# First bias of a top-2 mixture added on VectorE, and split expert weights kept in DRAM for the second mixture

## The reference, cut to what matters

```
logits = x @ gate_w.T + gate_b
top_vals, top_idx = top_k(logits, 2); routing = softmax(top_vals)
for e in range(8):
    h = x @ w1[e].T + b1[e]                       # 256 -> 512
    y = h[:, 0::2] * sigmoid(1.702 * h[:, 0::2]) * (h[:, 1::2] + 1.0)
    ye = y @ w2[e].T + b2[e]                      # 256 -> 256
    out = out + ye * sum(routing * (top_idx == e))
```

## Time and profile before

| | us |
|---|---|
| median of 3 runs | 2635.42 |
| lowest, highest | 2635.4, 2640.15 |
| the profiled execution, its own time | 2634.61 |
| its span, first to last instruction | 2632.8 |
| moe0: its start to the first tile | 0 to 62.02 |
| moe0: tile loop | 62.02 to 187.2 |
| moe1: its start to the first tile | 1001 to 1044.55 |
| moe1: tile loop | 1044.55 to 1173.0 |

### The profile page before, as it was taken

One profiled execution on the slowest core, in us unless ns is written; L12 is line 12 of the kernel. 1 busy time (PEld: TensorE's weight loads), 2 busy tenths in 40 slices (PEclk: granted clock), 3 DMA queues, 4 the chain that ended last, 5 costly groups with the idle time before them and its releaser, 6 DMA issues. The chain is left out here.

```text
span 2632.8 us, 44981 instructions
## 1 busy us (share of the span) xinstructions
PE 2357.4 (90%) x15959; PEld 1837.2 (70%) x15959; DVE 1699.6 (65%) x3422; ACT 1351.9 (51%) x2729; POOL 1133.2 (43%) x1015
## 2 busy tenths in 40 slices
PE   4985899999999994978989999889979999998799
PEld 3874555665666553866877777677778887886688
DVE  7548786776777716547555997879855545555443
ACT  4433345555555563433238886868655544444322
POOL 2553111211112111555316773746466677777232
PEclk9997899999999995998999999999999999999999
DMA  5224001000000003233000000000023333333200
GB/s 171 77 90 123 20 11 36 16 20 20 16 25 9 16 20 121 78 106 140 1 15 1 1 5 5 1 9 1 25 101 101 90 98 106 104 104 105 86 9 25
DMA packets 79941, 138.65 MB, mean 53 GB/s; under 512 B 27360, under 2 KB 48568, under 8 KB 78832
## 3 DMA queue, kind: packets, MB, share of 16 engines
q0 software_dynamic: 26512, 74.12, 9.4%
q1 hardware_dynamic: 53216, 61.65, 7.4%
HBM read 114.53 MB, written 20.94 MB: 51 GB/s over the span
## 5 line engine op out<-in xcount | busy, mean ns | idle before, releaser
L1634 ACT ACTIVATE PT<-ps 128x512 f32<-128x512 f32 (+3 forms) x640 | 300.5, 535 | 269.3 <-PE ps L1354 268.6
L2618 POOL DMA_INDIRECT KV<-kv_scratch,sidx x288 | 275.2, 956 | 113.4 <-issue 90.2
L35 PE MATMUL ps<-KIh,qih 128*128 128x512 f32 (+2 forms) x640 | 246.5, 385 | 45.9 <-DVE Isc L2118 35.3
L1496 DVE TENSOR_REDUCE xn<-ps 128x1 f32<-128x512 f32 x384 | 243.1, 684 | 67.8 <-PE ps L1339 65.6
L2181 POOL TENSOR_TENSOR part_sum<-part_sum,rlp 128x1024 f32<-128x1024 f32 (+7 forms) x138 | 241.0, 1746 | 95.8 <-ACT rlp L2011 94.7
L36 PE MATMUL ps<-KIl,qih 128*128 128x512 f32 (+2 forms) x640 | 239.3, 374 | 0.0
L37 PE MATMUL ps<-KIh,qil 128*128 128x512 f32 (+2 forms) x640 | 238.9, 373 | 0.0
L2118 DVE SCALAR_TENSOR_TENSOR Isc<-ps,iw,Isc 128x1024 f32<-128x1024 f32 (+7 forms) x198 | 191.9, 969 | 56.4 <-ACT ps L2035 52.8
L2035 ACT ACTIVATE ps<-ps,iwa 128x1024 f32<-128x1024 f32 (+7 forms) x222 | 188.0, 864 | 33.8 <-PE ps L37 33.4
L35 PEld LDWEIGHTS ps<-KIh,qih 128*128 128x128 f32 x640 | 124.3, 194 | 87.2 <-issue 65.8
L931 POOL TENSOR_TENSOR fyl<-fy,fyh 128x512 fp32r<-128x512 f32 x64 | 84.9, 1327 | 183.8 <-ACT fyh L811 183.8
(11 more groups left out here) (397 smaller groups left out, 6802.9 us busy)
## 6 DMA issues: line engine op xcount, KB each, us to landing
cs<-in_rope SPq DMA_DIRECT2D x20, 512.0 KB, 4.2
ycomb<-y_rows SPq DMA_DIRECT2D x16, 512.0 KB, 5.5
w1raw<-in_w SPq DMA_DIRECT2D x14, 512.0 KB, 5.5
KV<-kv_scratch,sidx POOLq DMA_INDIRECT x288
w2raw<-in_w SPq DMA_DIRECT2D x14, 256.0 KB, 6.4
xn_rows<-xnr SPq DMA_DIRECT2D x5, 512.0 KB, 4.9
wir<-in_wi SPq DMA_DIRECT2D x1, 2176.0 KB, 10.3
X<-in_x SPq DMA_DIRECT2D x1, 2048.0 KB
```

The costliest lines, as they stand in the source:

```text
L35: pe.matmul(out, lhs[0], rhs[0], start=start, stop=False)
L1496: v.tensor_reduce(part, o, AX_X, ALU.max).then_inc(a_free, 1)
L1634: s.activation(PT[:, rnd % 2, hh, lo:CH], ps[:, BANK[kind, u, j, r, hh % 2], lo:CH], ACT.Exp, scale=SCALE).then_inc(a_exp, 1)
L2618: g.indirect_dma_start(ring(k, m), None, a["kv_scratch"], bass.IndirectOffsetOnAxis(sidx[:, t % 2, at:at + 1], 0)).then_inc(rows_in[k % RB ...
```

## The change

It has two parts. **The first bias on DVE.** The matmul L703 goes. The bias b1 is transposed once (n == 0), stored as eight rows of 512 (`bias_up`), and in each mixture a DMA on SP spreads all eight rows to every partition (`bb1`, 16 KB a partition, 2 MB). In the loop DVE adds `bb1` of the tile's expert to the 512 columns in PSUM and writes `ub` in SBUF; DVE reads the expert's number with a register load of its own. The sigmoid, gt and y then read `ub` instead of PSUM. PE's U waits for `ub` of two tiles earlier instead of y. In the loop ACT does yh ahead of sig, and DVE does xgl, ub, yl, gt, y. `bb` holds only b2, so ACT clears 2048 elements instead of 6144, and the split and the bias rows have 256 elements instead of 768.

**The last four experts kept.** In moe0's loop SP stores the high and low parts of w1 and w2 of experts 4 to 7 to DRAM: four DMAs of 2, 2, 1 and 1 MB in rows of 16, 16, 8 and 8 KB a partition, the first behind result 4, the others 7 results apart. In moe1 experts 4 to 7 are not loaded raw, cast or subtracted; POOL issues four DMAs that read the kept parts back, right behind `ln_root` and ahead of its wait for the bias rows. PE's wait for low parts covers four experts (`whole_low`), and its wait `m_bg` also covers the kept parts (`pool_in`).

```diff
+        ub = sb("ub", [P, 2, F1], F32, moe_ctx)
-        gt = sb("gt", [P, 2, I], F32, moe_ctx)
-        y = sb("y", [P, 2, I], F32, moe_ctx)
+        gt, y = ub[:, :, 0:I], ub[:, :, I:F1]
...
+        def keeps(n):
+            return n == 0 and begun(1) > 0
+        def whole_low(n):
+            return E * (n + 1) if not begun(n) else E * n + WR + 1
+        def pool_in(n):
+            return 32 * (n + 1) + 64 * sum(begun(m) > 0 for m in range(n + 1))
+        def small_in(n):
+            return 64 * (n + 1) + 64 * sum(keeps(m) for m in range(n))
...
# SP, behind the stores of the rows and of bhi and blo
+            if n == 0:
+                sp.wait_ge(m_b1, 18)
+                sp.dma_start(b1_d, b1row[:]).then_inc(m_b1, 16)
+                sp.wait_ge(m_b1, 34)
+            sp.dma_start(bb1[:].rearrange("p e f -> p (e f)"), b1_d.rearrange("e f -> (e f)").partition_broadcast(P)).then_inc(m_b1, 16)
             for e in range(WR + 1, E):
-                weights(e)
+                if not begun(n):
+                    weights(e)
+            if keeps(n):
+                sp.wait_ge(m_wl, E * (n + 1))
+                for m, (kept, w) in enumerate(((kept1_d, w1h), (kept1_d, w1l), (kept2_d, w2h), (kept2_d, w2l))):
+                    sp.wait_ge(m_os, NT * n + 4 + 7 * m)
+                    sp.dma_start(kept[m % 2].bitcast(F32), w[:, WR + 1:].bitcast(F32)).then_inc(m_b, 16)
+                sp.wait_ge(m_b, small_in(n) + 64)
...
# ACT's loop: yh is put ahead of sig
+                    s.wait_ge(m_ub, 2 * A - 1)
+                    s.activation(sig[:, k % 2, :], ub[:, k % 2, 0:I], ACT.Sigmoid, scale=1.702).then_inc(m_sig, 1)
...
# DVE's loop
+                    if k == 0:
+                        v.wait_ge(m_b1, 34 + 16 * (n + 1))
+                        v.wait_ge(m_rt, routed("expert", n))
+                    e = v.value_load(te_u[0:1, k:k + 1], min_val=0, max_val=E - 1)
+                    v.wait_ge(m_up, A)
+                    if k >= 2:
+                        v.wait_ge(m_yt, A - 2)
+                    v.tensor_tensor(ub[:, k % 2, :], ps[:, U_BANK + k % 2, :], bb1[:, bass.ds(e, 1), :].rearrange("p a f -> p (a f)"),
+                                    ALU.add).then_inc(m_ub, 1)
# (yl)
+                    v.wait_ge(m_sig, A)
+                    v.tensor_tensor(gt[:, k % 2, :], ub[:, k % 2, 0:I], sig[:, k % 2, :], ALU.mult).then_inc(m_ub, 1)
+                    v.wait_ge(m_ub, 2 * A)
+                    v.scalar_tensor_tensor(out=y[:, k % 2, :], in0=ub[:, k % 2, I:F1], scalar=1.0, in1=gt[:, k % 2, :],
+                                           op0=ALU.add, op1=ALU.mult).then_inc(m_y, 1)
...
# POOL, behind ln_root
+            if begun(n):
+                for m, (kept, w) in enumerate(((kept1_d, w1h), (kept1_d, w1l), (kept2_d, w2h), (kept2_d, w2l))):
+                    g.dma_start(w[:, WR + 1:], kept[m % 2]).then_inc(m_bg, 16)
...
# PE
-            pe.wait_ge(m_wl, E * (n + 1))
-            pe.wait_ge(m_bg, 32 * (n + 1))
+            pe.wait_ge(m_wl, whole_low(n))
+            pe.wait_ge(m_bg, pool_in(n))
...
-                    pe.wait_ge(m_y, max(A - 2, 0) if r >= 2 else NT * n)
+                    pe.wait_ge(m_ub, 2 * (A - 2) - 1 if r >= 2 else 2 * NT * n)
...
-                    pe.matmul(o, selr[:], bb[:, bass.ds(e, 1), 0:F1].rearrange("p a f -> p (a f)"), start=False, stop=True).then_inc(m_up, 1)
+                    j.then_inc(m_up, 1)
```

More of the change, by code:

```diff
@@ L244, in build @@
         b1raw = sb("b1raw", [P, E, F1 // P], F32, share)
+        b1row = sb("b1row", [E, F1], F32, share)
         b2raw = sb("b2raw", [E, D], F32, share)
-        bhi = sb("bhi", [E, F1 + D], F32R, share)
-        blo = sb("blo", [E, F1 + D], F32R, share)
+        bhi = sb("bhi", [E, D], F32R, share)
+        blo = sb("blo", [E, D], F32R, share)
         share.close()
@@ L268, in build @@
         w1_dram, w2_dram = a["w1"], a["w2"]
+        kept1_d = nc.dram_tensor("kept_w1", (2, P, E - WR - 1, KD, F1), F32R, kind="Internal").ap()
+        kept2_d = nc.dram_tensor("kept_w2", (2, P, E - WR - 1, JI, D), F32R, kind="Internal").ap()
         m_w, m_wh, m_wl = [sem(f"m_w{k}") for k in range(WR + 1)], sem("m_wh"), sem("m_wl")
-        (m_b, m_bb, m_bg, m_io, m_rp, m_ra, m_rt, m_row, m_tr, m_xh, m_xl, m_up, m_sig, m_gt, m_y, m_yt, m_yh, m_yl, m_dn, m_os, m_x) = (
-            sem(x) for x in ("m_b m_bb m_bg m_io m_rp m_ra m_rt m_row m_tr m_xh m_xl m_up m_sig m_gt m_y m_yt m_yh m_yl m_dn m_os m_x").split())
+        (m_b, m_b1, m_bb, m_bg, m_io, m_rp, m_ra, m_rt, m_row, m_tr, m_xh, m_xl, m_up, m_sig, m_ub, m_y, m_yt, m_yh, m_yl, m_dn, m_os, m_x) = (
+            sem(x) for x in ("m_b m_b1 m_bb m_bg m_io m_rp m_ra m_rt m_row m_tr m_xh m_xl m_up m_sig m_ub m_y m_yt m_yh m_yl m_dn m_os m_x").split())
         m_rows = [sem("m_rows0"), sem("m_rows1")]
@@ L352, in moe_scalar @@
             s.wait_ge(consts, FIRST_IN)
[L353 to L357, removed]
+            s.activation(bb[:].rearrange("p e f -> p (e f)"), ident[:, 0:1].to_broadcast([P, E * D]), ACT.Copy, scale=0.0).then_inc(m_bb, 1)
+            s.wait_ge(m_b, small_in(n))
+            s.copy(bhi[:], b2raw[:]).then_inc(m_bb, 1)
+            if n == 0:
+                s.wait_ge(m_b1, 17)
+                s.copy(b1row[:], ps[0:E, CNT_BANK, :]).then_inc(m_b1, 1)
             for c in range(begun(n), NCH):
                 q = NCH * LNC[n] + c
-                if c >= 2:
-                    s.wait_ge(m_rp, PRODUCTS * n + c)
+                if c >= begun(n) + 2:
+                    s.wait_ge(m_rp, PRODUCTS * n + c - 1)
                 for k in range(KD):
@@ L370, in moe_scalar @@
             s.activation(gate[:], gap[:], ACT.Sigmoid).then_inc(m_ra, 1)
-            s.wait_ge(m_rp, PRODUCTS * n + NCH + 2)
+            s.wait_ge(m_rp, PRODUCTS * n + NCH + 1)
             s.copy(totb[:], ps[:, CNT_BANK, 0:1].to_broadcast([P, P])).then_inc(m_ra, 1)
-            for e in range(WR + 2 - (begun(n) > 0), E):
-                weights(e)
+            for e in range(WR + 2, E):
+                if not begun(n):
+                    weights(e)
             for i in range(NT + 3):
@@ L381, in moe_scalar @@
                     s.copy(xgh[:, i % 2].rearrange("p k t -> p (k t)"), ps[:, T_BANK + i % 2, 0:D]).then_inc(m_xh, 1)
[L382 to L386, removed]
                 if 2 <= i < NT + 2:
@@ L640, in logits @@
                                       start=t == CT * begun(n) and k == 0, stop=t == TILES - 1 and k == KD - 1)
[L641 to L646, removed]
+                i.then_inc(m_rp, 1 + (begun(n) if c == NCH - 1 else 0))
+            pe.wait_ge(m_b, small_in(n))
+            if n == 0:
+                pe.wait_ge(m_b1, 16)
+                for j in range(F1 // P):
+                    i = pe.transpose(ps[0:E, CNT_BANK, j * P:(j + 1) * P], b1raw[:, :, j], ident[:])
+                i.then_inc(m_b1, 1)
             for c in range(begun(n), NCH):
@@ L722, in moe_tensor @@
                                  w2l[:, bass.ds(e, 1), h, :].rearrange("p a f -> p (a f)")), h == 0, False)
-                    pe.matmul(o, selr[:], bb[:, bass.ds(e, 1), F1:F1 + D].rearrange("p a f -> p (a f)"), start=False, stop=True).then_inc(m_dn, 1)
+                    pe.matmul(o, selr[:], bb[:, bass.ds(e, 1), :].rearrange("p a f -> p (a f)"), start=False, stop=True).then_inc(m_dn, 1)
         ahead_ctx = ExitStack()
```

45 lines of the change are left out of this document (21 added, 24 removed).

## The result

The changed kernel takes **2660.19 us** (median of 4 runs, 2656.98 to 2663.47), the kernel before 2635.84 on the same chip (4 runs). The ratio is 1.0087, with a 95% interval of 1.0071 to 1.0102. I had forecast 2638.4 and a range of 2621 to 2653, so the result is outside the range on the slow side.

A forecast was written before the change was run, and what follows sets the result against it. The prediction took PE to bound both tile loops. From the profiled 2634.6 us, plus 0.8 to the median, it added -11 + 5.3 + 1.2 + 7.5 = +3.0, giving 2638.4 us, range 2621 to 2653.

The forecast's parts named there:

- What bounds the loop: Both tile loops: PE busy 120.6 of 125.2 and 121.6 of 128.5 us, so PE bounds; 2.88 us a tile.
- Part 1, -11: Both loops without the bias matmul: tile from 2.88 to near 2.74 us (estimates 2.65, 2.79, 2.72); -11 us.
- POOL: Loops: DMAs starting at random moments wait for DVE operations with two SBUF operands, 0.14 us a tile, giving 2.72.
- rival D: Loops: POOL's scatter meets gt or y in every tile, 3.0 us a tile, no gain; 2649.4 us, chance 0.17.
- Part 2, +5.3: moe0's loop: stores delay gathers, packets alternating one for one; 2.4 us per 2 MB store, 0.25 per 1 MB; +5.3.
- Part 3, +1.2: moe0's start: storing and spreading b1 moves expert 4's landing from 33.9 to 39.4; +1.2 us (0 to +6.4).
- E: moe0's start: the spread of b1 runs at half rate, +5.2 us; total 2643.6 us, chance 0.13.
- Part 4, +7.5: moe1's start: kept loads pass before expert 3, which comes 15.0 us later; first tile +7.1, second gather +0.4; +7.5 us.
- The variant with turns of 4 KB: moe1's start: kept parts get 4 KB a turn, expert 3 only 6.5 us later; 2629.9 us, chance within B's 0.24.
- B: moe1's start: rings favour SP's queue or share by bytes, -6.6 for +7.5; 2624.3 us, chance 0.24 with the 4 KB variant.
- C: Loops: PE stays the bound at 2.65 us a tile, gathers' slack takes the stores; 2626.1 us, chance 0.10.
- The rest, 0: The span outside moe0 and moe1: carried over unchanged, 0 us.

The follow-up runs named there:

- run 6: Kernel before, with TensorE's register load of a tile's expert number moved from behind T to behind the previous tile's U; 2628.34 us, ratio 0.9962.
- run 1: Changed kernel without the kept experts, so the bias part alone; 2641.11 us, ratio 1.002 to the kernel before.
- run 5: run 1 with TensorE's register load of the expert number moved behind the previous tile's U; 2626.29 us, ratio 0.9953 to the kernel before.
- run 10: Changed kernel with the edits of run 3, run 5 and run 7, and POOL issuing gathers ahead of the result wait and scatter; 2607.16 us, ratio 0.988.
- run 12: run 10 without the kept part; 2615.46 us, ratio 0.9892 to the kernel before.
- run 11: run 10 without the bias part, the first bias again by TensorE's product; 2618.1 us, ratio 0.9909 to the kernel before.
- run 2: Kernel before with only the kept part added, bias still a matmul; 2658.58 us, ratio 1.0099.
- run 4: Changed kernel with each store cut by expert into rows of 4 and 2 KB, pieces still issued together; 2660.13 us, ratio 1.0099 to the kernel before.
- run 3: Changed kernel with POOL issuing the kept loads only once expert 3's raw weights have landed; 2642.82 us, ratio 1.0024 to the kernel before.
- run 8: run 2 with the edits of run 3 and run 7, bias still a matmul; 2635.09 us, ratio 0.9982 to the kernel before.
- run 7: Changed kernel with the stores cut by expert into sixteen, one at every second result; 2651.48 us, ratio 1.0052 to the kernel before.

## Why the prediction was wrong

**What bounds the loop: wrong, and the first cause.** I read "PE is busy 120.6 of 125.2 us" as the bound and took the pace for PE's. Run 6 took 7.5 and 7.3 us out of the two loops without touching PE's work. Gaps of 0.3 to 0.7 us in some tiles are lost in a 96% share. My 2.88 us was the pace of tiles whose register load is hidden; the mean over before's loop is 120.2 / 38 = 3.16. The row that told it was in my hands, and I named the register load, but priced it as something the new chain would bring, not as what the loop already paid.

**Part 1, -11: wrong.** The step that failed is "2.65, 2.79 and 2.72 meet near 2.74". Measured in run 1: -0.6 and +0.3. I let an exposed register load cost 2.79 a tile at the worst, by a chain through Y. In run 1 tiles take 2.65 to 3.7 us, because the load starts only shortly before T, and a load that lasts 523 instead of 300 ns puts U off by that much more. PE's sequencer had lost part of its lead, as I had written, but the price was too low: the steps from T to U grew by 6.7 us in the first loop, most of the 9 us that 39 bias matmuls of 0.23 us take. That this is the cause is shown by run 5 (-6.4 and -8.8 us for the one move). The rest of the gain hung on POOL's order (runs 10 and 12). With both out of the way the part gives 6.7 and 6.6 us a loop (run 11 against 10), 13.3 in all, 0.17 a tile; so -11 was about the price of the part, but not in this kernel. The bound of 2.65 us a tile that I had given PE alone is what runs 10 and 12 reach. DVE's register load, which I counted as nothing, takes 0.30 us and 0.19 for the arithmetic in run 10, and the tiles of 2.65 us run all the same.

**POOL: the wait right, its timing and size wrong.** I had a scatter or gather meet DVE's operations with two SBUF operands at random. The runs show it otherwise:

```profile
89.80 0.96 POOL L661 DMA_INDIRECT xg<-xn_rows,id_in  x1 [0.30 <-issue]
...
90.82 0.42 DVE L619 SCALAR_TENSOR_TENSOR ub<-ub 128x256 f32<-128x256 f32 x1
91.07 1.04 POOL L673 DMA_INDIRECT y_rows<-osb,id_out  x1 [0.30 <-issue]
```

This is run 10. In its first loop all 34 scatters that the timeline shows between 70 and 168 us start inside y (L619), as rival D had it, with 0.04 to 0.28 us of y left, and they are longer by about what is left: 1.04 us with 0.17 left, 1.15 with 0.28, 0.99 with 0.04. (The gather of 1.54 in the earlier trace rows started with 0.58 us of L406 left.) So a scatter does wait for y's end, but it comes late in y and pays 0.17 us at most, not 0.42. The gathers start outside gt and y and stay at 0.96. The means are 1.07 and 0.96, with two gaps of 0.30 that makes 2.63 a tile, just under PE's 2.65, where I had 2.72. Rival D's price (3.0 a tile, each scatter held for a whole DVE operation) is refuted: tiles of 2.65 us run through both loops of runs 10 and 12. The Trainium skill (SBUF — State Buffer, SBUF: two separate sides) has the loser of the shared port pair blocked until the other's instruction is over. The scatters' lengths agree with that; the gathers, beside which gt runs at its usual 0.42 us, show no wait on either side.

**Part 2, +5.3: mechanism half right, size too small.** The loop lost 9.4 us (9.7 in run 2). The failed step is "Packets of the two queues alternate one for one". That came from rows of other stretches, in which neither queue had 2 MB of its own. Here 111 hardware packets passed between 88 and 92 and not one of the software queue. The wait behind the first 2 MB store was near my figure, 2.51 for 2.4 us. What I had not counted is that the scatters are held too: one issued in that store landed 7.3 us behind its issue (2.6 in the loop of run 5), and the results' four buffers with it. Nor had I counted PE's register load: it lasts 0.9 us in four tiles of this loop, each 1.4 to 3.2 us behind the issue of one of the four stores, but 0.54 at most in run 1 and 0.50 in run 10. The loop is 10.1 us longer than run 1's: T's waits for gathers (5.9 us) are 5.4 of it and the steps from T to U 2.1; the split of the other 2.6 stays open. The Trainium skill (DMA: Bandwidth & Descriptors, Queues, rings and completion order) has each engine change queue only when it has drained a whole packet, typically of 9 to 17 descriptors. Whether what the profile counts as a packet is one such packet or a part of it, no run here shows. A store of 2 MB in rows of 16 KB has 8 rows for each of 16 engines, an estimate, so if they went as one packet of the page's kind, nothing else would pass meanwhile, as from 88 to 92; the 39 software packets beside 44 hardware ones in the second store speak against it. The cause stays open, and so does why small rows let the software queue in earlier (run 4) and still helped nothing.

**Part 3, +1.2: right** (+1.2 and, in run 1, +1.3; E is out).

**Part 4, +7.5: right.** Expert 3 came 13.9 us late for my 15.0, the first U 6.4 for my 7.5, and run 3 shows the cause by taking it away. The one-for-one rule holds here, where both queues had megabytes waiting: 479 packets of each from 1024 to 1040. The variant with turns of 4 KB (6.5 us late) is out, and so is B. C is out as well: no loop with the stores as they were had tiles without waits.

**The rest, 0: wrong in the profile, probably in the main not caused by the change.** 9.9 us lie behind the last D of moe1, in unchanged code. That stretch took 1459.9 to 1462.0 us in the five profiled executions with a mean clock of 0.956, before's among them, and 1461.4 to 1471.8 in the nine at 0.949 to 0.954; the longest is run 8's, whose loops have the bias as before. One stretch of it shows what: the end of the select stage, about the same work, first in the trace of before and then in that of after. The granted clock of 0.84 is a mix of the two levels, 1.2 and 2.4 GHz:

```profile
2440.00:2480.00 40.00, 31.59 (x238) 25.72 (x234) 13.10 (x32) 9.43 (x32) 5.61 (x6) 1.00 0.09 27
```

```profile
2463.00:2507.00 44.00, 35.95 (x224) 29.07 (x224) 12.75 (x29) 9.43 (x32) 5.72 (x7) 0.84 0.08 23
```

In runs 1 to 3 the matmuls of the select stage's output product (`swo`) there take 383 ns on average as before, against 412 in the changed kernel's and 401 in run 12's. One and the same kernel moves by as much: of run 5's twelve executions, those at a mean clock of 0.955 to 0.956 took 2622 to 2624 us on average and the one at 0.949 took 2635. The kernel before took 2642 at 0.952, 2640 at 0.953, 2637 at 0.955 and 2634 at 0.956 (of the 31 executions beside runs 5 to 8). The changed kernel's four had 0.949 to 0.953. At 0.952 and 0.953 it took 2658.4 and 2657.0, 16 to 17 us above those of before at that clock, and the table's rows ahead of "the rest" add to 19.0. So some 16 to 19 us go with the change, and most of the others with the clock. Whether the change has a part in its lower clock is open: four executions don't say.

**The sum.** +1.2 and +6.4 where I had +1.2 and +7.5; +8.4 in the two loops where I had -5.7; 1.3 for the drains, which I had left out (y now comes a chain later). The loops are 14 us of the error, and the stretch behind moe1, with its clock, most of the rest.

## What to carry to other kernels

A busy share of 96% does not prove an engine the bound: look at how its period varies from tile to tile, and test it by moving what its sequencer does between instructions (here a register load) under work that is already queued. A bulk copy in the background of small gathers is priced by the largest burst in flight against the gathers' lead, not by its bytes: cut it in time, not only in size, and put it behind the loads that the critical path waits for. Take work off an engine only after finding what else is within a tenth of its period; here three things were (the register load, POOL's pair of DMAs, the landing of gathers), and each took the gain in turn.

## What the runs showed of the hardware that I had not expected

- A register load on TensorE: 0.30 us for the load in most tiles and up to 0.55, 0.15 for arithmetic and about 0.3 until the next weight load. Moving it under queued products gave 6.4 to 8.8 us in 39 tiles (runs 5 and 6). Close behind the 1 and 2 MB stores it took 0.9 us.
- The software queue got no packet for 4 us while a hardware store of 2 MB ran, though a scatter had been issued at 87.42 and a gather at 88.87.
- A scatter's issue that starts inside a DVE operation with two SBUF operands ends about as much later as that operation has left (1.04 us with 0.17 left, 1.15 with 0.28).
- The releaser of a PE gap can be named wrongly: "DVE y" before U, where moving the register load removed the gap.
